# A four-layer pipeline on one core: two batches share the banks of the spectra and of the gate stage, ScalarE squares the rectified units, and each engine gets a new order

## The reference, cut to what matters

```
stage a   q, kv = x @ W_q.T, x @ W_kv.T        # 16 heads of 16
          qf, kvf = normalised fft of each head
          kvf = cumsum(kvf over the tokens)
          out = ifft(qf * kvf).real @ W_o.T
stage g   scores of 8 experts: squares of select_weight . (x - mean_diff), over |x - mean_diff|
          gate = sigmoid(slope * (score - center)); the best expert of each token
          out = (1 - g) * x + g * (bias + degen(update(x - debias)))
stage b,e 16-head softmax attention over 256 tokens, heads of 16, then @ W_o.T
stage c   h = relu(x @ w1.T) ** 2              # w1, w2: ternary weights, 1024 hidden units
          out = rms_norm(h) @ w2.T
```

## Time and profile before

| | us |
|---|---|
| median of 3 runs | 843.16 |
| the profiled execution | 849.45 |
| its span, from first to last instruction | 847.4 |

### The profile page before, as it was taken

The page is one execution under the profiler, slowest core; times in us unless marked ns, Lnnn a source line. Parts: engine busy times, 40 slices in busy tenths (PEclk is TensorE's granted clock), DMA queues, the critical chain, the costliest instruction groups (busy, mean ns, idle before and its releaser), DMA issues.

```text
span 847.4 us, 14775 instructions
## 1 busy us (share of the span) xinstructions
PE 689.9 (81%) x5100; PEld 530.8 (63%) x5100; DVE 603.5 (71%) x1429; ACT 442.9 (52%) x897; POOL 410.6 (48%) x601
## 2 busy tenths in 40 slices
...
GB/s 191 62 0 14 0 149 11 140 14 137 15 150 20 144 15 149 20 144 15 149 22 142 16 150 22 143 22 143 22 142 16 135 23 129 38 115 14 1 13 12
DMA packets 298170, 60.57 MB, mean 71 GB/s; under 512 B 237352, under 2 KB 293616, under 8 KB 298096
## 3 DMA queue, kind: packets, MB, share of 16 engines
...
## 4 chain that ended last, share of the span: by engine, by line
PE 45%; DVE 36%; issue 6%; POOL 4%; ACT 4%; SPq 3%; DMA 3%; POOLq 0%; DVEq 0%; ACTq 0%
DVE nmax L1235 10%; PE pC L728 7%; PE pA L512 5%; PE pC L706 5%; DVE x L1040 4%; PE pS L681 3%; PE pA L539 3%; DVE spec L1079 3%; PE pA L498 3%; DVE ss L1069 2%; PE pS L631 2%; PE pB L605 2%; PE pA L555 2%; PE pA L589 2%; PE pA L570 2%
## 5 line engine op out<-in xcount | busy, mean ns | idle before, releaser
L1235 DVE TENSOR_REDUCE nmax<-pB 128x2 f32<-128x512 f32 x256 | 165.5, 675 | 21.8 <-PE pB L605 20.3
L861 ACT ACTIVATE pt<-pS 128x512 f32<-128x512 f32 x256 | 149.1, 608 | 12.4 <-PE pS L631 12.4
L631 PE MATMUL pS<-qT,kT 98*128 98x256 bf16 x512 | 92.6, 277 | 12.8 <-ACT pt L861 10.9
L605 PE MATMUL pB<-kT,qT 96*128 96x256 bf16 x512 | 96.6, 282 | 7.4 <-DVE nmax L1235 4.3
L1444 POOL TENSOR_TENSOR hid_lo<-hh,hid 128x512 fp32r<-128x512 f32 x64 | 81.8, 1279 | 6.1 <-POOL hh L1416 5.3
L1416 POOL TENSOR_TENSOR hh<-hr 128x512 f32<-128x512 f32 x64 | 72.4, 1132 | 20.2 <-ACT hr L889 20.1
L824 ACT COPY qkv<-pA 128x512 f32<-128x512 f32 x48 | 30.2, 630 | 93.6 <-PE pA L589 93.6
L706 PE MATMUL pC<-x3T,w1T 128*128 128x256 f32 x256 | 71.2, 309 | 6.5 <-DVE x3T_lo L1291 4.2
L1421 POOL TENSOR_TENSOR hsum<-hsum,hsq 128x512 f32<-128x512 f32 x48 | 60.9, 1270 | 30.1 <-ACT hsq L901 30.1
L657 PE MATMUL pO<-pt,v_ext 128*32 128x256 f32 x1024 | 70.3, 393 | 2.8 <-ACT pt L861 2.8
L1355 POOL TENSOR_SCALAR vea<-mva 128x2 f32<-128x2 f32 x16 | 3.6, 223 | 131.6 <-DVE mva L1036 131.6
...
## 6 DMA issues: line engine op xcount, KB each, us to landing
...
qT<-qk_scratch SPq DMA_DIRECT2D x96, 128.0 KB, 3.0
kT<-qk_scratch SPq DMA_DIRECT2D x96, 128.0 KB, 2.8
...
```

The source lines that it names most:

```text
L605: ins = pe.matmul(pB[h % 2][:, s * T:(s + 1) * T], qT[k][0:STACK, u * P:(u + 1) * P], kT[k][0:STACK, h * T:(h + 1) * T], start=True, stop= ...
L631: ins = pe.matmul(pS[h % 2][:, s * T:(s + 1) * T], kT[k][:, u * P:(u + 1) * P], qT[k][:, h * T:(h + 1) * T], start=True, stop=True)
L861: act.activation(pt[:, (h // 4) % 2, h % 4].rearrange("p s n -> p (s n)"), pS[h % 2][:], ACT.Exp, scale=HD ** -0.5).then_inc(S["probs"], 1)
L1235: dve.tensor_reduce(nmax[:, h * SIDES:(h + 1) * SIDES], pB[h % 2][:].rearrange("p (s k) -> p s k", s=SIDES), AX.X, ALU.max, negate=True).t ...
```

## The change

It does five things.

1. `c_h_g`, the square of the rectified units, is a ScalarE activation (Square) in place of a GpSimd product of `hr` with itself.
2. `raw_spec` becomes two buffers, by the parity of the batch, and `prodT` (the transposed products) lies in `prod` in place of a half of `raw_spec`.
3. In bank `pA[0]`, `a_xt` of batch i+1 waits only for `attn_read` of batch i-1, and `a_cum` of batch i waits for `proj_sb` of batch i+1: the first half of a batch's stage a is done between the second halves of its neighbours.
4. In bank `pA[1]`, `g_x1t` and `g_gate` of batch i come ahead of `g_x2t` and `g_qkv` of batch i-1, and these ahead of `g_mixt` and `g_mix` of batch i. The waits change with it. The scratch output of the sums of squares in `g_x1t_sb` goes to `mix` in place of `x2`.
5. All five lists of `ORDER` are new. `a_xt` of batch i is in turn i as before, `c_y` of batch i is in turn i + 6; on SyncE `g_out_2` stands ahead of `g_in_0`.

```diff
+    "e_score_8:+1 g_x1t e_out_1:+1 e_score_9:+1 e_score_10:+1 g_gate b_max_0:+1 b_max_1:+1 e_score_11:+1 "
+    "e_score_12:+1 g_x2t:+1 b_max_2:+1 e_out_2:+1 b_max_3:+1 e_score_13:+1 c_hid_2:+1 b_max_4:+1 "
+    "b_max_5:+1 g_qkv_0:+1 b_max_6:+1 b_max_7:+1 e_score_14:+1 e_score_15:+1 c_hid_3:+1 b_max_8:+1 "
+    "b_max_9:+1 g_qkv_1:+1 b_max_10:+1 e_out_3:+1 b_max_11:+1 a_xt:-1 w_gate b_max_12:+1 g_qkv_2:+1 "
+    "e_outt_0:+1 b_max_13:+1 b_max_14:+1 e_outt_1:+1 a_proj_0:-1 b_max_15:+1 a_proj_1:-1 w_turn_0:+1 "
+    "e_ont:+1 g_mixt c_ms:+1 b_maxt_t:+1 a_cum e_vt e_wo:+1 c_y:+1 e_score_0 a_prt e_score_1 g_mix "
+    "e_score_2 c_x3t a_attn w_turn_1:+1 e_score_3 e_score_4 c_hid_0 e_out_0 e_score_5 e_score_6 c_hid_1 "
+    "e_score_7 "
+
+    "e_exp_0:+1 a_prt_sb:+1 e_exp_1:+1 a_squares c_x3t_sb:+1 e_exp_2:+1 e_vt_sb:+1 e_exp_3:+1 e_exp_4:+1 "
+    "c_relu_0:+1 c_h_0:+1 e_exp_5:+1 e_exp_6:+1 e_out_sb_0:+1 w_turn_sb_1:+2 e_exp_7:+1 e_exp_8:+1 "
+    "c_hi_0:+1 g_x1t_sb e_exp_9:+1 e_exp_10:+1 e_out_sb_1:+1 e_exp_11:+1 c_hsq_0:+1 g_x2t_sb:+1 "
+    "c_relu_1:+1 e_exp_12:+1 c_h_1:+1 c_hi_1:+1 c_hsq_1:+1 c_relu_2:+1 e_exp_13:+1 c_h_2:+1 g_qkv_sb_0:+1 "
+    "c_hi_2:+1 e_exp_14:+1 e_out_sb_2:+1 c_hsq_2:+1 e_exp_15:+1 c_relu_3:+1 g_exp c_h_3:+1 g_qkv_sb_1:+1 "
+    "c_hi_3:+1 c_hsq_3:+1 e_out_sb_3:+1 a_xt_sb:-1 g_qkv_sb_2:+1 g_first:+1 a_proj_sb_0:-1 w_turn_sb_0:+1 "
+    "a_proj_sb_1:-1 g_mixt_sb e_ont_sb:+1 g_mid:+1 b_keep "
+
+    "w_gate_prod w_qkv_split_0 a_sums w_sign_0_0:+1 w_sign_0_1:+1 g_norm2:+1 g_gate1_0 b_max_read_0:+1 "
+    "g_gate1_1 b_max_read_1:+1 b_max_read_2:+1 g_x2t_lo:+1 b_max_read_3:+1 g_gate1_2 g_gate1_3 "
+    "b_max_read_4:+1 b_max_read_5:+1 g_gate1_4 a_inverse g_gate1_5 b_max_read_6:+1 b_max_read_7:+1 "
+    "a_spectra_0 b_max_read_8:+1 a_spectra_1 b_max_read_9:+1 b_max_read_10:+1 g_gate2_0 b_max_read_11:+1 "
+    "g_gate2_1 b_max_read_12:+1 g_gate2_2 g_gate2_3 a_xt_lo:-1 w_qkv_split_1 w_qkv_split_2 w_scale_0 "
+    "w_sign_0_2:+1 w_sign_0_3:+1 w_bias:+1 w_scale_1:+1 g_gate2_4 e_outt_den_0:+1 g_gate2_5 "
+    "b_max_read_13:+1 e_outt_norm_0:+1 b_max_read_14:+1 e_outt_den_1:+1 g_gate2_6 b_max_read_15:+1 "
+    "e_outt_norm_1:+1 g_gate2_7 g_rest:+1 b_maxt_0:+1 b_maxt_1:+1 c_ms_read:+1 b_maxt_sb:+1 a_even "
+    "w_sign_1_0:+1 g_low:+1 a_cross w_sign_1_1:+1 e_res:+1 a_products_0 w_sign_1_2:+1 e_bn:+1 "
+    "a_products_1 w_sign_1_3:+1 e_mean:+1 c_res:+1 e_norm:+1 c_bn:+1 g_res2 c_mean:+1 g_bn c_x3t_lo "
+    "g_mean a_res1 a_bn a_mean a_norm1 "
+
+    "c_lo_1:+1 c_add_2:+1 c_lo_2:+1 c_add_3:+1 c_lo_3:+1 c_hsum:+1 c_rms:+1 e_pow:+1 g_pow2 c_pow:+1 "
+    "a_pow1 c_norm:+1 a_root_0:-1 a_root_1:-1 a_root_2:-1 c_lo_0 a_root_3:-1 a_root_4:-1 c_add_1 "
+
+    "g_out_2:+2 g_in_0:+2 w_load_fc:+1 w_load_proj:+1 w_load g_in_1:+2 g_in_2:+2 g_v_out:+2 p_load "
+    "g_v_in:+2 c_store:+2 g_out_0:+1 b_rows:+1 g_out_1:+1 "
...
-        raw_spec = sb("raw_spec", [P, SIDES, 512])
+        raw_spec = [sb(f"raw_spec{k}", [P, SIDES, 512]) for k in range(2)]
...
-        prodT = raw_spec[:, 1, :]
+        prodT = prod[:].rearrange("p s c n -> p (s c n)")
...
             def a_xt(i, k):
                 pe.wait_ge(S["x_in"], nth(i, PER["x_in"], 16))
-                if has(i):
-                    pe.wait_ge(S["attn_read"], before(i, PER["attn_read"]))
+                if has(i, 2):
+                    pe.wait_ge(S["attn_read"], before(i, PER["attn_read"], back=2))
+                elif has(i):
+                    pe.wait_ge(S["proj_sb"], before(i, PER["proj_sb"]))
...
             def a_cum(i, k):
                 pe.wait_ge(S["spectra"], nth(i, PER["spectra"], 2))
+                if i + 1 < BATCHES:
+                    pe.wait_ge(S["proj_sb"], nth(i + 1, PER["proj_sb"], 2))
+                else:
+                    pe.wait_ge(S["attn_read"], before(i, PER["attn_read"]))
...
             def g_x1t(i, k):
                 pe.wait_ge(S["x1_done"], nth(i, PER["x1_done"], 2))
                 if has(i):
-                    pe.wait_ge(S["qkv_sb"], before(i, PER["qkv_sb"]))
+                    pe.wait_ge(S["ffn_read"], before(i, PER["ffn_read"]))
...
             def g_mixt(i, k):
                 pe.wait_ge(S["mix_done"], nth(i, PER["mix_done"], 1))
+                if has(i):
+                    pe.wait_ge(S["qkv_sb"], before(i, PER["qkv_sb"]))
...
             def g_x2t(i, k):
                 pe.wait_ge(S["x2_done"], nth(i, PER["x2_done"], 2))
+                if i + 1 < BATCHES:
+                    pe.wait_ge(S["gate_read"], nth(i + 1, PER["gate_read"], 1))
...
-                if s == 0:
-                    if has(i):
-                        act.wait_ge(S["attn_ready"], before(i, PER["attn_ready"]))
-                act.copy(raw_spec[:, s, :], pA[0][:]).then_inc(S["proj_sb"], 1)
+                if s == 0:
+                    if has(i, 2):
+                        act.wait_ge(S["products"], before(i, PER["products"], back=2))
+                act.copy(raw_spec[k][:, s, :], pA[0][:]).then_inc(S["proj_sb"], 1)
...
-                if has(i):
-                    act.wait_ge(S["xb_copied"], before(i, PER["xb_copied"]))
-                if has(i):
-                    act.wait_ge(S["x2t_ready"], before(i, PER["x2t_ready"]))
                 for s in range(SIDES):
                     if s:
                         act.wait_ge(S["x1_sq"], nth(i, PER["x1_sq"], s))
-                    act.activation(x2[:, s, :], x1[k][:, s, :], ACT.Square,
+                    act.activation(mix[:].rearrange("p s n -> p (s n)"), x1[k][:, s, :], ACT.Square,
                                    accum_out=s2[:, s:s + 1]).then_inc(S["x1_sq"], 1)
...
+            def c_h(i, g):
+                act.wait_ge(S["relu_done"], nth(i, PER["relu_done"], g + 1))
+                if g >= 2:
+                    act.wait_ge(S["hsq_done"], nth(i, PER["hsq_done"], g - 1))
+                    act.wait_ge(S["lo_done"], nth(i, PER["lo_done"], g - 1))
+                elif has(i):
+                    act.wait_ge(S["hsq_done"], before(i, PER["hsq_done"], g + 3))
+                    act.wait_ge(S["lo_done"], before(i, PER["lo_done"], g + 3))
+                act.activation(hh[:, g % 2, :], hr[:, g % 2, :], ACT.Square).then_inc(S["h_done"], 1)
...
-                pool.tensor_tensor(hh[:, g % 2, :], hr[:, g % 2, :], hr[:, g % 2, :],
-                                   ALU.mult).then_inc(S["h_done"], 1)
```

More of the change, by code:

```diff
@@ L98 @@
 ORDER = (
[20 rows of a table removed]
-    "c_ms_read b_maxt_0 b_maxt_1 g_rest a_res1 b_maxt_sb a_bn g_low e_res a_mean e_bn e_mean a_norm1 "
-    "e_norm c_res "
[4 rows of a table removed]
[25 rows of a table added]
+    "g_mean a_res1 a_bn a_mean a_norm1 "
[4 rows of a table added]
 ).split()
@@ L186, in mega_kernel @@
         ones = sb("ones", [P, P])
-        minus_half = sb("minus_half", [P, 2 * UNITS])
+        minus_half = sb("minus_half", [P, SIDES])
         xa = [sb(f"xa{k}", [P, SIDES, D]) for k in range(2)]
@@ L770, in a_xt_sb, with a_proj_sb @@
                 act.copy(flat(xT[:]), pA[0][:]).then_inc(S["xt_sb"], 1)
-            def a_proj_sb(i, s):
+            def a_proj_sb(i, k, s):
                 act.wait_ge(S["proj_ready"], nth(i, PER["proj_ready"], s + 1))
                 if s == 0:
-                    if has(i):
-                        act.wait_ge(S["attn_ready"], before(i, PER["attn_ready"]))
-                act.copy(raw_spec[:, s, :], pA[0][:]).then_inc(S["proj_sb"], 1)
+                    if has(i, 2):
+                        act.wait_ge(S["products"], before(i, PER["products"], back=2))
+                act.copy(raw_spec[k][:, s, :], pA[0][:]).then_inc(S["proj_sb"], 1)
             def a_squares(i, k):
@@ L781, in a_squares @@
                 if has(i):
-                    act.wait_ge(S["prt_ready"], before(i, PER["prt_ready"]))
-                act.activation(spec[:].rearrange("p s a b n -> p (s a b n)"), raw_spec[:].rearrange("p s n -> p (s n)"),
+                    act.wait_ge(S["crossed"], before(i, PER["crossed"]))
+                act.activation(spec[:].rearrange("p s a b n -> p (s a b n)"), raw_spec[k][:].rearrange("p s n -> p (s n)"),
                                ACT.Square).then_inc(S["squares"], 1)
@@ L916, in _ @@
             for n in range(SIDES):
-                steps[f"a_proj_sb_{n}"] = lambda i, k, n=n: a_proj_sb(i, n)
+                steps[f"a_proj_sb_{n}"] = lambda i, k, n=n: a_proj_sb(i, k, n)
             for n in range(2):
@@ L924, in _ @@
                 steps[f"c_hi_{n}"] = lambda i, k, n=n: c_hi(i, n)
+                steps[f"c_h_{n}"] = lambda i, k, n=n: c_h(i, n)
                 steps[f"c_hsq_{n}"] = lambda i, k, n=n: c_hsq(i, n)
@@ L1075, in a_inverse, with a_spectra @@
                 dve.reciprocal(rn[:].rearrange("p s m -> p (s m)"), root_t[:]).then_inc(S["norm_rs"], 1)
-            def a_spectra(i, s):
+            def a_spectra(i, k, s):
                 dve.wait_ge(S["norm_rs"], nth(i, PER["norm_rs"], 1))
@@ L1080, in a_spectra @@
```

(16 more changed lines are left out.)

9 lines of the change are left out of this document (removed), and 24 rows, old and new, of the table ORDER.

## The result

The changed kernel took 839.5 us (median, 835.9 to 844.1) against 843.75 for the kernel before in the same rounds: a ratio of 0.9944, 95% interval 0.9917 to 0.9970. That is faster by 0.56%, some 4 us, where 43 had been forecast.

A forecast was written before the change was run, and what follows sets the result against it. Bound: TensorE and VectorE alternating, tied by one stage a and one stage g through single banks each turn. First `c_y` at 241, nine turns of 39.2 and 210 of drain gave a span of 804, so 800 us; range 778 to 836.

The forecast's parts named there:

- `c_h` to ScalarE: Four products a turn leave GpSimd: 0 in full turns, about 2.5 us off each of the last two intervals.
- Banks and order: New lists and bank use in full turns: the turn falls from 42.3 to 39.2 us, between 37.4 and 42.3.
- My walk: One full turn followed step by step through VectorE and TensorE with the trace's lengths: 38.8 us, 39.2 with small waits.
- Port: VectorE's SBUF port lock with GpSimd: `g_norm2` and `a_spectra` get 1.6 us a turn shorter.
- rival D: Remaining GpSimd steps still lock the same VectorE steps, whose half-turn is 1 us longer: 813 us, chance 0.09.
- Fill: Start of the run, deeper pipeline and weights ahead on VectorE: first `c_y` at 241 us, bounds 231 and 252.
- Drain: After nine full turns: six intervals of 38.5, 37, 35.5, 33, 27, 25 and a tail of 14, 210 us.
- SyncE at 0: Loads queued behind `g_out_2`, which waits for `g_low`, cost nothing a turn; bounds 0 and +1.5 us.
- B: ScalarE's second `a_proj_sb` copy is late for `a_cum`, 850 us at 4.4 us late; slower, chance 0.10.
- C: Thinner turns in the fill hold TensorE's clock low for at most one more turn: 810 us, chance 0.06.
- A: New waits from shared banks and from loads hold the turn at 41 us: 825 us, chance 0.21.
- no change: Time within 0.2% of the kernel before, chance 0.04.

The follow-up runs named there:

- run 1: The changed kernel with `c_h` back on GpSimd as a product, new banks and order kept: 871.8 us, ratio 1.031 to the kernel before.
- run 2: The kernel before with only `c_h` moved to ScalarE, old banks and order kept: 833.7 us, ratio 0.986.
- run 5: The changed kernel with seven of the gate's small steps moved in VectorE's list, away from GpSimd's `c_add` and `c_lo`: 829.6 us, ratio 0.981.
- run 6: The changed kernel with the one-time preparation of the feed-forward weights one to two turns later in the fill: 836.6 us, ratio 0.989.
- run 3: The changed kernel with GpSimd's `c_lo` and `c_add` cut to 8 of 512 columns for every batch but the first: 818.1 us, ratio 0.968.

## Why the prediction was wrong

The span was forecast at 804 and was 835.4. The 31 us are the fill (+7), nine full turns (9 x 1.1 = +9.9) and the drain (+14.7).

**`c_h` to ScalarE: wrong.** "In a full turn neither is the bound, so this costs 0" took busy time for slack. The move was worth 2.3 us a turn in the new order, 0.7 in the old, and without it the changed kernel loses (871.8). That the time came out faster, as forecast, rests on this term, which I had put at 0 in the full turns, and so is in part luck.

**Banks and order: wrong, and what the gain was built on.** I let the new order, with the port, take the turn from 42.3 to 39.2 by freeing VectorE's waits. Alone it leaves the turn at 42.56 (run 1), since GpSimd's steps, spread over the old turn, are in one row in the new one; with `c_h` moved it takes 1.3 us off, where 3.1 had been forecast. My walk followed VectorE and TensorE and never laid GpSimd's queue beside them. (Its terms up to the last `e_outt_norm` also add up to 20.3, not 20.5.) The order needs `c_h` moved: with `c_h` on ScalarE the order is worth 1.3 us a turn (41.62 to 40.30, 12 us in nine turns), but pays some 21 us in the fill (248.0 against 227.2), and run 2 beats the changed kernel by 6 us.

**Port: the mechanism right, its place wrong.** I took -1.6 for `g_norm2` and `a_spectra`. They gave 2.1, `g_norm2` all but wholly (0.45 us against the forecast 0.5), and the gate's small steps, which I had priced at 3.5 us in all, took 2.8 more (2.1 over all sixteen). That is rival D's mechanism on steps that it didn't name. Run 5 shows that this is the error of the turn: with these steps moved away most turns are 38.9, under the forecast 39.2. VectorE's first half took 22.3 us (from 502.4 to 524.7) and not 20.5, and `c_y` started 27.5 us into the turn and not 26.3. The other half was right: `c_y` to the next `a_norm1` took 12.9, forecast 12.5.

**Fill: the direction right, 7 us short.** The first `a_norm1` (77.3, forecast 78), `g_norm2` (110.4, 107) and maxima (148.6, 145) were near. The rest, 99.4 us to `c_y` in place of 96, has two longer turns in it (2 x 1.1). But the cause that I named, weights on VectorE, was worth 2.6 us (run 6); the rest of the longer fill I put down to the depth, which is argued and not shown.

**Drain: wrong by 14.7, the largest term.** The gain that the order was to bring here didn't come. All behind the tenth `c_y` took 235.4 us before and was forecast at 210; `c_h` alone brought it to 225.0 (run 2), and the order added nothing (224.7). The products that leave GpSimd gave what I had taken for them or more: from run 1 to the changed kernel the last two intervals fell by 2.9 us each (34.9 to 32.0 and 28.8 to 25.9), against 2.5. But I had also let every interval start from the forecast turn and shorten as soon as a stage is gone. The first two (40.9 and 40.0) hardly do, since the chain of maxima and gate steps goes on without stage a, and in run 3, with the gate's steps short, they don't either (39.0 and 38.9, turn 38.66). The interval before the last is 32.0 and not 27: ScalarE is busy 19.49 us of it, and the chain alternates between exponentials, `hr`, `hh` and `hid` on ScalarE and products on TensorE. In the old order, with `c_h` moved, it was 31.8.

**SyncE at 0** was right at a turn of 40.3, by little: the last load is issued 40.0 us into the turn (at 542.35) and takes 2.7 to land, and `b_max_0` wants it at 43.4. In run 5, with most turns at 38.9, the loads held single turns. The prediction's own terms (25.9 + 14.5 + 2.8) also add up to 43.2, not to 42.3, and 43.2 is behind the 42.4 at which it wanted them. **Rivals:** B's wait of `a_cum` for `a_proj_sb` isn't among the waits of the turn, and C's low clock didn't come (0.80 from 145 to 180 us, 1.00 in full turns). D named the mechanism and priced it at 813 with 0.09. The time came out above A's 825 and past the slow end of the range, 836, next to "no change", where I had put the least chance, 0.04.
